# Row maxima of two heads from two halves of TensorE's rows, with the causal mask moved into the maximum instruction

## The reference, cut to what matters

```
q       = einsum('bld,dhk->blhk', x, Wq)                 # 8 x 1024 tokens, D = 256, 16 heads of 64
latent  = einsum('bld,dc->blc',  x, Wkv_down)            # 64 wide
k, v    = latent @ Wk_up, latent @ Wv_up
attn    = softmax(where(key <= query, q k / sqrt(64), min), axis=key)
x       = layernorm(x + (attn v) Wout)
...                                                       # router over 32 experts, capacity 320, top 1
x       = layernorm(x + expert_ffn(x))
```

## Time and profile before

| | |
|---|---|
| median of 3 runs | 2971.61 us (2959.61 to 2977.6) |
| the profiled execution | 2956.08 us, span 2954.3 us |
| mean granted clock of TensorE | 0.954 |
| busy: PE, DVE, ACT, POOL | 2750.7 (93%), 1555.7 (53%), 1010.4 (34%), 1522.2 (52%) us |
| matmuls | 14120, of which 1536 row scores (L612) and 1024 of their masks (L615) |

### The profile page before, as it was taken

The page is one execution under the profiler, slowest core; times in us unless marked ns, Lnnn a source line. Parts: engine busy times, 40 slices in busy tenths (PEclk is TensorE's granted clock), DMA queues, the critical chain, the costliest instruction groups (busy, mean ns, idle before and its releaser), DMA issues.

```text
span 2954.3 us, 38198 instructions
## 1 busy us (share of the span) xinstructions
PE 2750.7 (93%) x14120; PEld 1710.8 (58%) x14120; DVE 1555.7 (53%) x3346; ACT 1010.4 (34%) x1496; POOL 1522.2 (52%) x1162
## 2 busy tenths in 40 slices
PE   7999999999999999999999999999999999959996
PEld 5555565556555565566555655566555655546664
DVE  3555546554655456554655465545655465325553
ACT  2333424342434334432334234423343243212222
POOL 0555545653565446654565356545664465513444
PEclk8899999999999999999999999999999999969998
DMA  8000001100010002000100011000100010034551
GB/s 213 15 19 16 18 8 41 32 16 11 26 47 16 12 11 62 15 15 8 56 17 15 11 29 44 16 11 16 58 15 15 10 42 19 8 118 130 158 157 64
DMA packets 97576, 119.05 MB, mean 40 GB/s; under 512 B 12992, under 2 KB 76488, under 8 KB 97392
## 3 DMA queue, kind: packets, MB, share of 16 engines
q1 hardware_dynamic: 90224, 99.98, 12.6%
q0 software_dynamic: 7168, 16.64, 1.5%
HBM read 46.91 MB, written 37.90 MB: 29 GB/s over the span
## 4 chain that ended last, share of the span: by engine, by line
PE 85%; DVE 9%; issue 2%; ACT 2%; POOL 1%; DMA 1%; SPq 0%; POOLq 0%; ACTq 0%; DVEq 0%
PE value_ps L663 19%; PE turned_ps L639 10%; PE row_ps L612 10%; PE turned_ps L645 9%; PE misc_ps L680 8%; PE misc_ps L559 7%; PE turned_ps L768 5%; PE misc_ps L672 4%; PE row_ps L615 2%; PE turned_ps L641 2%; DVE unit_max L994 2%; PE value_ps L781 2%; PE misc_ps L781 2%; DVE q_hl L980 2%; DVE q_hl L979 1%
## 5 line engine op out<-in xcount | busy, mean ns | idle before, releaser
L421 POOL TENSOR_TENSOR sums<-sums,probs 128x1024 f32<-128x1024 f32 (+3 forms) x512 | 827.7, 1617 | 543.8 <-ACT probs L846 520.6
L846 ACT ACTIVATE probs<-turned_ps 128x1024 f32<-128x1024 f32 (+3 forms) x768 | 622.6, 811 | 1228.2 <-PE turned_ps L645 1198.6
L994 DVE TENSOR_REDUCE unit_max<-row_ps 128x1 f32<-128x512 f32 (+3 forms) x1024 | 554.8, 581 | 273.1 <-PE row_ps L612 264.3
L663 PE MATMUL value_ps<-probs,lat_keys 128*64 128x512 f32 (+3 forms) x3072 | 622.2, 529 | 1.2 <-ACT probs L846 1.2
L645 PE MATMUL turned_ps<-q_max,lat_lo 65*128 65x512 f32 (+3 forms) x1536 | 613.2, 400 | 2.3 <-DMA q_max<-max_rows 2.3
L639 PE MATMUL turned_ps<-q_hl,lat_hi 128*128 128x512 f32 (+3 forms) x1536 | 597.3, 389 | 0.0
L612 PE MATMUL row_ps<-lat_hi,q_hl 128*128 128x512 f32 (+3 forms) x1536 | 469.1, 376 | 60.4 <-DVE unit_max L994 57.4
L639 PEld LDWEIGHTS turned_ps<-q_hl,lat_hi 128*128 128x128 f32 x1536 | 297.8, 194 | 200.0 <-issue 167.0
L417 POOL TENSOR_TENSOR sums<-probs 128x768 f32<-128x768 f32 (+1 forms) x128 | 268.8, 2100 | 200.6 <-ACT probs L846 200.3
L612 PEld LDWEIGHTS row_ps<-lat_hi,q_hl 128*128 128x128 f32 x1536 | 290.9, 197 | 114.4 <-DVE unit_max L994 82.8
L663 PEld LDWEIGHTS value_ps<-probs,lat_keys 128*64 128x64 f32 x3072 | 195.7, 143 | 213.1 <-issue 168.1
(11 more groups left out here) (169 smaller groups left out, 2645.8 us busy)
## 6 DMA issues: line engine op xcount, KB each, us to landing
q_max<-q_hl SPq DMA_DIRECT2D x256, 128.0 KB
slots_x<-headsT SPq DMA_DIRECT2D x40, 258.0 KB, 9.8
ex_x<-slots_x SPq DMA_DIRECT2D x64, 129.0 KB, 3.4
x_in<-in_L_attn_x_bld SPq DMA_DIRECT2D x8, 1024.0 KB
layer_out<-x_in SPq DMA_DIRECT2D x8, 1024.0 KB, 4.4
ex_w<-in_L_ffn_w_gate SPq DMA_DIRECT2D x32, 256.0 KB, 2.8
ex_w<-in_L_ffn_w_up SPq DMA_DIRECT2D x32, 256.0 KB, 3.0
ex_w<-in_L_ffn_w_down SPq DMA_DIRECT2D x32, 256.0 KB, 3.5
```

Of the source, the lines that this page charges most:

```text
L421: nc.gpsimd.tensor_tensor(sums[c][:, :, q0:BANK], sums[c][:, :, q0:BANK], now[:, :, q0:BANK], ALU.add).then_inc(added, 1)
L663: mm = nc.tensor.matmul(value_ps[h * LD:(h + 1) * LD, q0:BANK], lat_keys[b % 2][:, j, :], probs[:, n % NPROBS, h, q0:BANK], start=(j == 0) ...
L846: nc.scalar.activation(probs[:, n % NPROBS, :, q0:BANK], turned_ps[n % 2][:, :, q0:BANK], ACT.Exp).then_inc(exp_done, 1)
L994: ins = nc.vector.tensor_reduce(dst, row_ps[n % 2][:, 0:width], AX.X, ALU.max, negate=True)
```

## The change

It does four things. The units of query tiles 4 to 7 are ordered so that the two heads of one (i, k) stand together. Each row matmul takes only the partitions of its head's half (`rows`), which hold the high part of its queries, so its depth is 64 instead of 128 and the low part of the queries no longer enters the maximum. The mask matmul is gone. For units that end on the diagonal the maximum is now `tensor_tensor_reduce`: it adds a float32 constant `future` (zero, with -1e30 above the diagonal in its last 128 columns), negates, writes a bf16 row that nobody reads (`masked_row`), and gives the minimum. A semaphore `sums_turned`, unused before, is replaced by `kept`, unused as well, and a lambda `kept_by` is defined and not called.

```diff
     UNITS = ([(h, i, 0) for i in range(HPB) for h in range(2)]
-             + [(h, i, k) for i in range(HPB, NT) for h in range(2) for k in range(2)])
+             + [(h, i, k) for i in range(HPB, NT) for k in range(2) for h in range(2)])
...
-        future_bf = sb("future_bf", [P, P], BF16, attn)
+        future = sb("future", [P, BANK], F32, attn)
+        masked_row = [sb(f"masked_row{i}", [P, BANK], BF16, attn) for i in range(2)]
...
-            nc.gpsimd.memset(future_bf[:, :], 0.0).then_inc(const_ready, 1)
+            nc.gpsimd.memset(future[:, :], 0.0).then_inc(const_ready, 1)
...
-            nc.gpsimd.affine_select(out=future_bf[:, :], in_=future_bf[:, :], pattern=[[-1, P]], compare_op=ALU.is_ge,
-                                    fill=MASKED, base=0, channel_multiplier=1).then_inc(const_ready, 1)
+            nc.gpsimd.affine_select(out=future[:, BANK - P:], in_=future[:, BANK - P:], pattern=[[-1, P]],
+                                    compare_op=ALU.is_ge, fill=MASKED, base=0, channel_multiplier=1
+                                    ).then_inc(const_ready, 1)
...
                 dst = row_ps[n % 2]
-                last = k1 == (i + 1) * P
-                mm = nc.tensor.matmul(dst[:, 0:k1 - k0], q_hl[gp % 2][:, h, i * P:(i + 1) * P], lat_hi[b % 2][:, k0:k1],
-                                      start=True, stop=not last)
-                if last:
-                    mm = nc.tensor.matmul(dst[:, k1 - k0 - P:k1 - k0], ident_bf[:, :], future_bf[:, :], start=False, stop=True)
-                mm.then_inc(rows_full, 1)
+                rows = slice(h * LD, (h + 1) * LD)
+                nc.tensor.matmul(dst[:, 0:k1 - k0], q_hl[gp % 2][rows, h, i * P:(i + 1) * P], lat_hi[b % 2][rows, k0:k1],
+                                 start=True, stop=True).then_inc(rows_full, 1)
...
-                ins = nc.vector.tensor_reduce(dst, row_ps[n % 2][:, 0:width], AX.X, ALU.max, negate=True)
-                ins.then_inc(max_done, 1)
+                if k * BANK + width == (i + 1) * P:
+                    nc.vector.tensor_tensor_reduce(masked_row[n % 2][:, 0:width], row_ps[n % 2][:, 0:width], future[:, BANK - width:],
+                                                   scale=-1.0, scalar=-MASKED, op0=ALU.add, op1=ALU.min, accum_out=dst
+                                                   ).then_inc(max_done, 1)
+                else:
+                    nc.vector.tensor_reduce(dst, row_ps[n % 2][:, 0:width], AX.X, ALU.max, negate=True
+                                            ).then_inc(max_done, 1)
```

More of the change, by code:

```diff
@@ L57, in build_layer @@
     assert NU == 2 * NSLOT
+    kept_by = lambda n: n // NSLOT * NT + sum(on_diagonal(t) for t in range(n % NSLOT + 1))
     NPROBS = 6
@@ L188, in build_layer @@
         added = sem("added")
-        sums_turned = sem("sums_turned")
+        kept = sem("kept")
         inverse_done = sem("inverse_done")
```

## The result

| | before | after |
|---|---|---|
| median, both on the same chip in turn | 2972.53 us | 3062.14 us (3054.12 to 3079.85) |
| ratio, 95% interval | | 1.0313 (1.0264 to 1.0362) |
| profiled execution, its span | 2956.08, 2954.3 us | 3066.37, 3064.5 us |
| mean granted clock of the span | 0.954 | 0.902 |
| matmuls | 14120 | 13096 |

The change costs 90 us where I forecast 25, and the time lies just outside the range (3060).

A forecast was written before the change was run, and what follows sets the result against it. TensorE was taken to bound the kernel (85% of the chain). Per pass -0.15 us on TensorE and waits and +0.36 on VectorE, times 63, gave +13 us; clock +12; on 2971.6 that made 2997 us, range 2945 to 3060.

The forecast's parts named there:

- What goes from TensorE and what comes: TensorE, per pass: halved row streams and dropped masks save 3.67 us; seventeen shape switches and pair starts add 3.45 us.
- serial weight loads: Rival, row matmul pairs: the two row halves load weights one after the other, 83 us on top, 3080; chance 0.10.
- pairs that do not run together: Rival, row matmul pairs: the second waits for the first, 132 us on top, 3129; chance 0.04.
- The net of a pass: TensorE and its waits in slots 3, 0 and 10: near -0.15 us per pass, before VectorE's new instruction.
- up to 2x: Skill's rule for two row tiles at contraction 64 or less; the prediction equated it with the 3.67 us savings.
- hidden weights: Rival, TensorE: weight loads behind a shape switch are hidden, 118 us less, 2879; chance 0.06.
- VectorE's new instruction: 16 of 24 maxima, +0.06 us each, counting six times per pass in slots 3, 10 and 0: +0.36 us.
- VectorE pays nothing extra: Rival, slots 3, 10 and 0: no added VectorE cost and clock falls as often as now, -9 us, 2962; chance 0.20.
- The clock: Behind slot 10's stall: 7 more passes have a fall to 1.2 GHz, +12 us; bounds none to 42 us.
- the clock falls in every pass: Rival, behind slot 10's stall: every pass has its fall, 13 + 42 = +55 us, 3027; chance 0.15.

The follow-up runs named there:

- e1: After with the row matmuls at full depth (all 128 partitions) again, new order and mask in the maximum kept: 2911.86 us, ratio to before 0.9828.
- e7: After with both heads' row matmuls in the same lower half of the partitions, so a pair cannot run together: 3059.66 us, ratio to before 1.0354.
- e2: After with the plain reduction for every unit, the mask left out of the maximum: 3030.37 us, ratio to before 1.0215.
- e3: After with eight extra full-depth matmuls, results discarded, in slot 10's wait in 47 passes: 2942.39 us, ratio to before 0.9919.
- e4: Before with eight extra full-depth matmuls, results discarded, in slot 10's wait in 47 passes: 2917.17 us, ratio to before 0.9840.
- e5: e1 with eight extra full-depth matmuls, results discarded, in slot 10's wait in 47 passes: 2870.04 us, ratio to before 0.9717.
- e11: After with the values of slots 8 and 9 issued ahead of slot 10's row matmuls: 2906.05 us, ratio to before 0.9771.
- e8: After with the eight extra matmuls of e3 at depth 64, same place and columns: 3000.90 us, ratio to before 1.0111.
- e9: e1 with the values of slots 8 and 9 issued ahead of slot 10's row matmuls: 2816.88 us, ratio to before 0.9482.

## Why the prediction was wrong

**What goes from TensorE and what comes: right in kind.** No mask matmul is left. In the timeline of PE of after, slot 3 and slot 5 of the pass in which the stall was shown:

```profile
889.00 0.84 PE L616 MATMUL row_ps<-lat_hi,q_hl 64*128 64x512 f32 x2
889.78 1.08 PE L673 MATMUL misc_ps<-sums,ones_f 128*64 128x512 f32 x4
```
```profile
894.41 0.33 PE L616 MATMUL row_ps<-lat_hi,q_hl 64*128 64x128 f32 x2
894.67 0.50 PE L640 MATMUL turned_ps<-q_hl,lat_hi 128*128 128x512 f32 x1
895.00 0.39 PE L646 MATMUL turned_ps<-q_max,lat_lo 65*128 65x512 f32 x1
```

A pair of 128 columns leads the next start by 0.26, and the score matmul behind it lasts 0.50, as I had it from the earlier trace rows: weights in the open. The Trainium skill, "TensorEngine Tiling (Array Packing)", section "Key Properties", says that row tiles load and run side by side, and the trace agrees: the second matmul of a pair starts 3 ns behind the first where both are ready, and 1536 loads of 196 ns cover 176.2 us, 0.115 each:

```profile
L616 PEld LDWEIGHTS row_ps<-lat_hi,q_hl 64*128 64x128 f32 x1536 | 176.2, 196 | 256.4 <-issue 121.7 <-DVE unit_max L996 66.8 <-DVE unit_max L1000 36.7
```

In slot 3 (the 0.84 above, where such a pair takes 0.50 elsewhere) and in slot 10 it starts 0.17 and 0.48 behind on the median, since it waits for the second maximum, as forecast. The rivals of serial weight loads (+83 us) and of pairs that do not run together (+132) fall with the undisturbed pass of 32.84 us.

**The net of a pass: the right number, in part by luck.** I had -0.15 us from TensorE and the waits; -0.15 was measured (32.83 against 32.98). The terms behind it were each too large. From before to e1, which loses the masks (and gets the new order and maximum), a pass gains 0.97 us (33.00 to 32.03), where I had 1.57. From e1 to e7, where the row matmuls get the half shape but do not run together, it loses 2.11 (to 34.14), where I had 3.4 for the switches. From e7 to after, where they do run together, it gains 1.30 (to 32.84), where I had 2.10. These are lengths of passes, so what lay in a wait is not in them. The three errors cancel. Two smaller slips are in the sum: 18 x 0.23 is 4.14 and not 4.19, and the "up to 2x" that I called the whole 3.67 is the 2.10 of it. The rival of hidden weights (1.87 us less) comes out neither in the length of a pass nor in the 0.50 of the score matmul above, and the switches cost more than the halves bring.

**VectorE's new instruction: priced right, placed wrong.** I took +0.06 each between 0 and 0.17, thus +0.36 per pass. It is 3 ns over the reduction at 512 columns and has a read of the accumulator of 83 ns beside it. The Trainium skill, "VectorE: DVE Perf Modes", section "Two Vector instructions with no wait between them", calls such an operation two instructions; the trace shows both. But the next maximum starts at 908.90 together with the read, and the plain reduction makes a plain pass no shorter (34.37 for 34.39, e2): +0.36 was 0, and "VectorE pays nothing extra", the rival I gave 0.20, had the structure right: -9 us.

**The clock: the step that failed.** "... so more passes should have their fall. Bounds: none more, or all of some 25 passes that I take to be without one (25 x 1.7 = 42 us). I take 7: +12 us." For a plain pass the place was right: the fall starts right behind the stall of slot 10, and filling the stall removes it. The number of falls rose from 42 to 64, 22 more, near the upper bound and not 7 (I had taken today's to be 50 to 65); the passes without any low time went from 21 to 9 of 63. What neither value held is their length: I priced each at one stretch of 3.4 us, but 23 of the 64 last over 5 us and hold 335 of the 481 us. The bound was built for one fall per pass and left out that the low clock can persist over half a pass. In place of the +12 us the profiles show 305 us more at the low clock, about 123 us of time. So the rival "the clock falls in every pass" (3027) had the direction and lacked the same thing; it missed by 35 us. The term also looked at the plain passes alone, while in after the first three passes of a sequence hold 38 of its 61 us at the low clock (13 of 22 in before), and e3 still has 20 there. There not every fall follows a stall: behind a wait that ends at 788.1, in the second pass shown above, comes a fall of 3.4 us, but the next one, 13.7 us from 796.7 on, begins 8.6 us after that wait with TensorE at work throughout. What starts such a fall was not followed.

**The sum, by the profiles.** The loop grew by 114.2 us: -9 of structure, and 123 with 305 us more at the low clock, 0.40 us for each. The single fall of before gives 1.7 us in 3.4, 0.5 for each; in the heavier passes some low time lies in waits. The 4 us that the start-up ended earlier give the 110 of the whole. That 0.40 was fitted to this pair; it then gives 36 us for the 90 us between e3 and e4, with 36 measured, and 34 for the 84 between e3 and e5, with 33 left of 83.3 when 0.80 x 63 is taken off.

**What is shown and what is not.** Shown: most of the loss is low clock (e3 takes the time at 1.2 GHz from 481 to 166 us, and the ratio to before from 1.031 to 0.992; against e4, with the same additions, 25 us remain); in the plain passes it starts with the stall (e3, e11); half depth and its pairs are what makes it frequent and long (e1, 191 us, with the same maxima and a stall of 1.25 us for 1.04). The depth of added matmuls by itself counts (e8). Not separated: how much of e1's 290 us is depth, how much two matmuls running as one, and how much the switches' gaps. e7 takes only the second away and gives 222 us, but in doing so it doubles the streaming and shortens the wait.

## What to carry to other kernels

Where TensorE is the bound, list its stalls before you make its work thinner: fewer and shallower matmuls ahead of a stall can pay less than the clock that falls behind it. Price the clock not by the number of falls alone but by how long one may last (17.1 us here, where a plain one had 3.4), and let the range reach there. The cure was a matter of order: ready work issued ahead of the instruction that waits, worth about 156 us on after (e11) and 95 us on e1 (e9).

## What the runs showed of the hardware that I had not expected

- The granted clock stays at 1.2 GHz for 17.1 us while TensorE is busy 97% of them (834.30 to 851.40).
- The same additional columns at depth 64 leave 317 us at the low clock, at depth 128 166 us (profiled executions of e8 and e3; 3000.9 against 2942.4 us of time).
- Matmuls whose result is thrown away, put into a wait, make a kernel faster: before by 1.6%, after by 3.8% (e4, e3).
- Two halves of the rows side by side, 512 columns or fewer each, lose to one matmul of full depth after the other, 32.84 against 32.03 us per pass, when they stand among matmuls of the full shape.
